# Expert down-projections of a mixture-of-experts block: from one fp32 product to three split fp32r products, two units later

## What is computed

```python
shared_out = silu(xf @ sw1) * (xf @ sw3) @ sw2
s = sigmoid(xf @ router_w.T)
_, topk_idx = top_k(s + router_bias, 2)
...
h = gelu(einsum('nd,edh->neh', xf, ew1), approximate=False)
y = einsum('neh,ehd->ned', h, ew2)
routed_out = einsum('ned,ne->nd', y, comb)
return (shared_out + routed_out).reshape(B, T, C)
```

## Time and profile before

| | us |
|---|---|
| median of 3 runs | 232.91 (232.39 to 233.5) |
| the profiled execution | 230.98 |
| its span, first to last instruction | 229.2 |
| PE busy | 207.9 (91%) |
| DVE busy | 157.3 (69%) |
| ACT busy | 137.9 (60%) |
| POOL busy | 107.5 (47%) |

### The profile page before, as it was taken

The page is one execution under the profiler, slowest core; times in us unless marked ns, Lnnn a source line. Parts: engine busy times, 40 slices in busy tenths (PEclk is TensorE's granted clock), DMA queues, the critical chain, the costliest instruction groups (busy, mean ns, idle before and its releaser), DMA issues.

```text
span 229.2 us, 4496 instructions
## 1 busy us (share of the span) xinstructions
PE 207.9 (91%) x1538; PEld 120.0 (52%) x1538; DVE 157.3 (69%) x333; ACT 137.9 (60%) x280; POOL 107.5 (47%) x208
## 2 busy tenths in 40 slices
PE   7998979989998989999899999899998999999970
PEld 7764555435564645546454554466664455645520
DVE  6688877849899899989994030664548655556654
ACT  2899464878877778778778877334341533534330
POOL 8787997023506379582965156144003802020203
PEclk9999955999999999999999999999999999999998
DMA  4391654384410000009000350000090010541011
GB/s 154 107 258 31 167 166 104 99 307 104 103 27 6 3 6 4 9 3 366 10 3 6 140 233 0 3 1 0 3 366 0 3 47 1 182 186 46 3 44 48
DMA packets 10422, 19.19 MB, mean 84 GB/s; under 512 B 1952, under 2 KB 7008, under 8 KB 9760
## 3 DMA queue, kind: packets, MB, share of 16 engines
q1 hardware_dynamic: 8976, 17.06, 22.7%
q10 hardware_dynamic: 1040, 1.05, 1.3%
q0 software_dynamic: 384, 0.79, 1.3%
HBM read 12.80 MB, written 1.11 MB: 61 GB/s over the span
## 4 chain that ended last, share of the span: by engine, by line
PE 68%; DVE 18%; ACT 7%; issue 4%; ACTq 1%; POOL 0%; POOLq 0%; DVEq 0%
PE ring L800 14%; PE pv_bank L826 10%; PE max_bank L960 9%; DVE top L672 8%; PE sum_bank L960 4%; PE ring L782 3%; PE ring L780 3%; PE ring L781 3%; ACT probs_mem L570 3%; PE max_bank L809 3%; PE pv_bank L834 2%; DVE hid L750 2%; PE misc_bank L882 1%; ACT xt L645 1%; PE misc_bank L780 1%
## 5 line engine op out<-in xcount | busy, mean ns | idle before, releaser
L672 DVE TENSOR_REDUCE top<-max_bank 128x2 f32<-128x512 f32 x128 | 81.0, 682 | 10.7 <-PE max_bank L809 10.4
L570 ACT ACTIVATE probs_mem<-ring 128x512 f32<-128x512 f32 x128 | 70.0, 596 | 19.4 <-PE ring L800 17.8
L800 PE MATMUL ring<-qstack,kstack 32*128 32x256 f32 x256 | 45.5, 336 | 6.4 <-ACT probs_mem L570 3.7
L809 PE MATMUL max_bank<-kstack,qstack 32*128 32x256 f32 x256 | 44.4, 338 | 1.1 <-DVE top L672 0.8
L800 PEld LDWEIGHTS ring<-qstack,kstack 32*128 32x128 f32 x256 | 29.3, 190 | 27.1 <-ACT probs_mem L570 16.1
L826 PE MATMUL pv_bank<-probs_mem,v 128*18 128x256 f32 x512 | 41.4, 397 | 0.4 <-ACT probs_mem L570 0.4
L750 DVE TENSOR_TENSOR hid<-xt,gates_mem 128x512 f32<-128x512 f32 x32 | 22.5, 703 | 24.0 <-ACT xt L645 24.0
L645 ACT ACTIVATE xt<-ring 128x512 f32<-128x512 f32 x32 | 19.1, 598 | 32.4 <-PE ring L782 32.4
L960 PE MATMUL max_bank<-hid,wf 128*128 128x512 f32 x60 | 32.0, 614 | 1.7 <-DVE hid L750 1.4
L809 PEld LDWEIGHTS max_bank<-kstack,qstack 32*128 32x128 f32 x256 | 28.3, 190 | 5.9 <-POOL kstack L475 1.8
L780 PE MATMUL ring<-yt_hi,wf_lo 128*128 128x512 f32 x40 | 31.3, 782 | 0.0
(11 more groups left out here) (191 smaller groups left out, 333.2 us busy)
## 6 DMA issues: line engine op xcount, KB each, us to landing
gates_mem<-gate_scratch SPq DMA_DIRECT2D x4, 2048.0 KB, 7.2
kstack<-gates_mem SPq DMA_DIRECT2D x36, 64.0 KB, 2.1
qstack<-gates_mem SPq DMA_DIRECT2D x24, 64.0 KB, 2.1
wf<-w_ffn_dram SPq DMA_DIRECT2D x1, 1408.0 KB, 6.3
xs<-x_dram SPq DMA_DIRECT2D x4, 256.0 KB, 5.4
xt<-x_t_dram SPq DMA_DIRECT2D x3, 256.0 KB, 4.4
qstack<-gates_mem POOLq DMA_DIRECT2D x12, 64.0 KB, 2.3
out_dram<-xs SPq DMA_DIRECT2D x3, 256.0 KB, 2.3
```

The lines of the kernel that those rows point to most:

```text
L570: nc.scalar.activation(probs[:, i % 2, s_heads(s)[r], :], ring_of(("scores", 2 * s + r))[:, :], ACT.Exp, scale=SCALE).then_inc(probs_made, 1)
L672: dve.tensor_reduce(top[:, m_heads(m)[r], t, :], max_bank[(2 * m + r) % NMAX][:, :].rearrange("p (h k) -> p h k", h=2), AX.X, ALU.max).the ...
L800: ins = mm(ring_of(("scores", 2 * s + r))[:, kt * S:(kt + 1) * S], kstack[rows, t, k:k + P], qstack[rows, t, b * S:(b + 1) * S], start=Tru ...
L809: ins = mm(max_bank[(2 * m + r) % NMAX][:, qt * S:(qt + 1) * S], qstack[rows, t, q:q + P], kstack[rows, t, b * S:(b + 1) * S], start=True, ...
```

## The change

Units 16 to 36 (`PARTED`) get a new job `parts`, in slot u + 1, and their down moves from slot u + 2 to slot u + 4. In `parts`, ACT copies `hid` of unit u to the fp32r buffer `hid_hi`, and POOL subtracts: `hid_lo` = `hid` - `hid_hi`. The down then is three fp32r products from these and from the split `ew2` (`e2_hi`, `e2_lo`), in place of one float32 product. `ew2` is split by POOL in eight pieces of 128 columns (`split e2`, slots 50 to 57). Of two jobs put in one slot the earlier put stands first, so in slot k ACT finds `parts` of unit k-1 ahead of the gelu of unit k. `hid` moves into the memory of `probs`, `hid_hi` and `hid_lo` into that of `kstack`, each four buffers. Units 37 to 39 and 0 to 15 keep the float32 down and the two slots. `accT`, `finT` and `norm2` of groups 1 and 2, whose last units (23 and 31) are parted, move two slots back.

```diff
+PARTED = range(NE + NG * NSH, NG * (NSH + NE) - 3)
+NPB = 4
+LAG, LAG_PARTED = 2, 4
...
+    for n in range(DOWN_PIECES):
+        put(18 + 2 * PIECES + n, ("split e2", n))
...
     for u in range(NUNITS):
         put(NHALF + u, ("unit", u))
-        put(NHALF + u + 2, ("down", u))
+        put(NHALF + u + (LAG_PARTED if u in PARTED else LAG), ("down", u))
+        if u in PARTED:
+            put(NHALF + u + 1, ("parts", u))
...
-        s = NHALF + last_of(g)
+        s = NHALF + last_of(g) + (LAG_PARTED - LAG if last_of(g) in PARTED else 0)
...
+        hid = probs_mem[:, 0:NHB * GT].rearrange("p (n t) -> p n t", n=NHB)
+        hid_hi, hid_lo = (kstack[:, i, 0:NPB * GT].rearrange("p (n t) -> p n t", n=NPB) for i in range(2))
...
+        def wait_hid_read(eng, u):
+            if u in PARTED:
+                eng.wait_ge(lo_made, u - PARTED.start + 1)
+            else:
+                eng.wait_ge(down_made, down_at[u])
...
+                    if kind == "split e2":
+                        c, e2 = slice(n * P, (n + 1) * P), slice(E2 + n * P, E2 + (n + 1) * P)
+                        pool.tensor_scalar(e2_hi[:, c], wf[:, e2], 1.0, None, ALU.mult).then_inc(e2_hi_made, 1)
+                        pool.wait_ge(e2_hi_made, n + 1)
+                        pool.tensor_tensor(e2_lo[:, c], wf[:, e2], e2_hi[:, c].bitcast(F32), ALU.subtract).then_inc(e2_split, 1)
+                    if kind == "parts":
+                        i = n - PARTED.start
+                        pool.wait_ge(hi_made, i + 1)
+                        pool.tensor_tensor(hid_lo[:, i % NPB, :], hid[:, n % NHB, :], hid_hi[:, i % NPB, :].bitcast(F32),
+                                           ALU.subtract).then_inc(lo_made, 1)
...
+                    if kind == "parts":
+                        wait_hid(act, b)
+                        n = b - PARTED.start
+                        if n == 0:
+                            act.wait_ge(pv_made, NHALF)
+                        if n >= NPB:
+                            act.wait_ge(down_made, down_at[b - NPB])
+                        nc.scalar.copy(hid_hi[:, n % NPB, :], hid[:, b % NHB, :]).then_inc(hi_made, 1)
...
+                        if b == 0:
+                            dve.wait_ge(pv_made, NHALF - 2)
                         if b >= NHB:
-                            dve.wait_ge(down_made, b - NHB + 1)
+                            wait_hid_read(dve, b - NHB)
...
+                        if b in PARTED:
+                            if b == PARTED.start:
+                                pe.wait_ge(e2_split, DOWN_PIECES)
+                            i = b - PARTED.start
+                            pe.wait_ge(lo_made, i + 1)
+                            c = slice((n - NSH) * P, (n - NSH + 1) * P)
+                            three(acc_bank[g][:, :], e2_hi[:, c], e2_lo[:, c], hid_hi[:, i % NPB, :], hid_lo[:, i % NPB, :],
+                                  False, b == last_of(g)).then_inc(down_made, 1)
```

More of the change, by code:

```diff
@@ L55 @@
 SPLIT = 512 + NE * P
+DOWN_PIECES = 8
 W1, W3, E1, W2, E2, RW = 0, 256, 512, 512 + NE * P, 512 + NE * P + 256, 512 + 2 * NE * P + 256
@@ L180, in build_layer @@
         rw_parts = sb("rw_parts", [P, 2, NE], F32R)
+        e2_hi = sb("e2_hi", [P, NE * P], F32R)
+        e2_lo = sb("e2_lo", [P, NE * P], F32R)
         ident = sb("ident", [P, P])
@@ L236, in build_layer @@
         comb_t = sb("comb_t", [NE, 2, S])
-        hid = sb("hid", [P, NHB, GT])
+        hid = probs_mem[:, 0:NHB * GT].rearrange("p (n t) -> p n t", n=NHB)
+        hid_hi, hid_lo = (kstack[:, i, 0:NPB * GT].rearrange("p (n t) -> p n t", n=NPB) for i in range(2))
         acc_t = xt[:, 0:GT]
@@ L274, in build_layer @@
         rw_split, w_hi_made, w_split = sem("rw_split"), sem("w_hi_made"), sem("w_split")
+        e2_hi_made, e2_split, hi_made, lo_made = sem("e2_hi_made"), sem("e2_split"), sem("hi_made"), sem("lo_made")
         up_made, act_made, sh_read, hid_dve, down_made = (
@@ L310, in build_layer @@
         staged = [u for u in uses if u[0] in ("q", "k")]
+        downs = [u for slot in slots for kind, u in slot.jobs if kind == "down"]
+        down_at = {u: n + 1 for n, u in enumerate(downs)}
         ring_uses = []
@@ L648, in _ @@
                         if t0 == 0:
-                            act.wait_ge(down_made, last_of(g) + 1)
+                            act.wait_ge(down_made, down_at[last_of(g)])
                             if g:
@@ L957, in _ @@
                                 pe.wait_ge(max_taken, 2 * NHALF)
[L958 to L961, removed]
+                        if b in PARTED:
[6 more added lines that the diff above has]
+                                  False, b == last_of(g)).then_inc(down_made, 1)
+                        else:
+                            wait_hid(pe, b)
+                            c = W2 + n * P
+                            mm(acc_bank[g][:, :], wf[:, c:c + P], hid[:, b % NHB, :], start=b == first_of(g),
+                               stop=b == last_of(g)).then_inc(down_made, 1)
                     if kind == "finT":
```

## The result

The kernel with the change takes 250.53 us (median of 6 runs, 247.82 to 252.63) against 233.2 (6 runs): a ratio of 1.0741, interval 1.067 to 1.0812. Its profiled execution took 247.82, with a span of 246.1, so 16.9 more than the 229.2 of before. Runs that were disturbed, on either side of a comparison, are left out of the ratios and of the times given for the experiments; the profiled executions of E1 and E2 were among them, and their stages are not read.

What follows compares the result with a forecast made beforehand. The bound was to move from PE to a loop through ACT, POOL and DVE of 2.53 us a unit: 16.0 to product 36 plus 1.2 at the end, 17.2 on 232.91, gives 250.1 us, range 237 to 254.

Steps and rivals of the forecast that it cites:

- rival A: Units 16 to 36: POOL's subtraction always precedes the next gate product, 2.53 us a unit; +17 us (15 to 20); chance 0.54.
- The loop: Gate product to next: hand-over 0.05, ACT copy 0.58, hand-over 0.08, POOL subtraction 1.27, product's remainder 0.55; 2.53 us a unit.
- The sum: Products 16 to 36 at 2.53 a unit, plus 0.5 net for finT and routing: product 36 ends 16.0 us later.
- B: POOL falls one unit behind after a delayed subtraction; loop 1.87, +5 us, 238; chance 0.30 with what lies between.
- The end: From product 36's end to the last down's start: 6.05 us instead of 4.86, so 1.2 more.
- C: PE's clock falls to its lower level because of idle time; 7 us more than rival A, 257; chance 0.08.
- Down as three products: PE, units 16 to 36: 0.85 becomes 0.72, gaining 0.13 us a unit, 2.7 us over 21 units, if PE sets the pace.
- The split of ew2: POOL's eight pieces, 8.8 us, mostly fit its waiting around y; one piece 1.1 late of 1.66 to spare; cost 0.
- A sign that was wrong: Units 17 to 36 of the profile after: the chain of waits goes through ACT, POOL and DVE; no size given.

Runs made afterwards that it cites:

- E1: Kernel before with only the float32 down of units 16 to 36 two slots later (lag of four), no split: 229.52 us, ratio 0.987 to before.
- E2: Changed kernel with ACT's copy and POOL's subtraction put behind the next unit in the slot: 238.64 us, ratio 1.028 to before.
- E5: Changed kernel with copy behind the next unit and POOL filling zeros instead of subtracting, low part of hid left out: 233.41 us, ratio 1.006 to before.
- E9: E5 with the transposes and load of group 3's gates (combT) two slots later: 232.72 us, ratio 1.007 to before.
- E3: Changed kernel with POOL's subtraction replaced by two zero fills that read nothing from SBUF, low part of hid left out: 238.96 us, ratio 1.028 to before.
- E10: E8 with the transposes and load of group 3's gates (combT) two slots later, full computation: 230.80 us, ratio 0.998 to before.
- E7: Kernel before with only the float32 down of units 16 to 36 one slot later (lag of three), no split: 229.47 us, ratio 0.989 to before.
- E4: Changed kernel with POOL's subtraction of 512 columns done as two of 256: 243.42 us, ratio 1.045 to before.
- E8: E2 with the subtraction on DVE, behind the product, instead of POOL, full computation: 234.18 us, ratio 1.011 to before.

## Why the prediction was right

Slower was forecast, by rival A, at a loop of 2.53 and 250.1 us; 250.53 came.

- **The loop.** The forecast had 0.05 + 0.58 + 0.08 + 1.27 + 0.55. The rows show 0.03 from product to copy, 0.69 from copy to subtraction (0.62 and 0.07), 1.27 and 0.54: 2.53. The copy from SBUF, bounded by 0.50 and 0.68, took 0.62 where 0.58 was put, and the hand-over from DVE less than was put. Unit spacings of 2.54 to 2.56 follow where nothing else disturbs.
- **The sum.** From the start of product 16 to the end of product 36 the forecast was 35.82 + 16.0 = 51.8; the rows give 231.26 - 179.26 = 52.0. From the end of product 17 on it is 48.68 against 19 x 2.53 = 48.07, so 0.6 where 0.5 net was put. That this size came out so well is luck: its parts, units from 1.87 to 2.99, were not worked out.
- **B, for short stretches.** It came as its condition had it, and after two units A was back, by the narrow margin worked out there. In after, DVE and POOL behind the last routing steps:

```profile
196.72 0.69 DVE L795 TENSOR_TENSOR probs_mem<-xt,gates_mem 128x512 f32<-128x512 f32 x1 [1.18 <-ACT xt L680]
198.59 0.72 DVE L795 TENSOR_TENSOR probs_mem<-xt,gates_mem 128x512 f32<-128x512 f32 x1 [1.18 <-ACT xt L680]
200.50 1.76 DVE L795 TENSOR_TENSOR probs_mem<-xt,gates_mem 128x512 f32<-128x512 f32 x1 [1.19 <-ACT xt L680]
...
197.48 4.24 POOL L504 TENSOR_TENSOR kstack<-probs_mem,kstack 128x512 fp32r<-128x512 f32 x3
```

POOL is one unit behind, two products take about 0.7 and stand 1.87 and 1.91 apart. The last of the three subtractions ends at 201.72, so with its usual 1.27 it started at about 200.45: 1.14 after the product that had ended at 199.31, where 1.12 was worked out. The product came at 200.50, 1.19 after, where 1.18 was. POOL was ahead by 0.05, and the product took 1.76. That the falls back to A come with products of 1.76 to 1.81 had not been put into the sum; with the shorter units of B they nearly cancel, as the 0.5 net allowed.

- **The end** was mis-sized: 1.2 was put, and from the end of product 36 to that of the last down it is 7.38 against 5.98, so 1.40. Product 39 did not follow 38 at once; it waited 0.46 for its gelu.
- **C** did not come on the pace of the units: from 215 to 230 the granted clock is 1.00 with PE idle for 5.9 of 15 us. The granted clock was 0.50, so 1.2 GHz, from about 209.5 to 213 and from 230 to 233.4, the first time just behind a wait of PE of 2.08 for the copy of an accumulator, the second time before such a wait, again of 2.08, was over. The argument against C, that the new gaps are shorter, was weaker than it looked: in the earlier trace rows the clock fell within the idle time of 1.40, not behind it. PE in after, at the first of them, and the window behind it:

```profile
209.13 0.77 PE L1020 MATMUL misc_bank<-ident,xt 128*128 128x128 f32 x4 [2.08 <-ACT xt L696]
```

```profile
210.00:215.00 5.00, 5.00 (x17) 3.93 (x17) 3.80 (x11) 2.18 (x5) 1.81 (x2) 0.71 0.00 0
```

The mean clock of 0.71 is part 1.2, part 2.4 GHz. The first fall cost nothing to speak of: the products of 211.09 and 216.14 are two units apart, 5.05 or 2.53 each, with the finT of group 1 between them. The second stands ahead of unit 39's up; that it made the 0.46 is likely, but no run took it away.

- **Down as three products** gives PE what was said and a little more: 1.39 a unit (E5) where 6 x 0.24 = 1.44 was put, against 1.57.
- **The split of ew2** was rightly taken at 0: y ended 0.6 later than before, at 127.31, and PE's transposes of it started at 127.73, still 0.42 behind it.
- **A sign that was wrong**: the chain was to go through ACT, POOL and DVE. It shows no POOL, for the reason given above.

The stages of the runs divide the loss. With the reads of POOL taken out, 50.64 becomes 38.80, so they cost 11.84; the copy ahead of the gelu is worth another 2.07 (E5), or 4.27 with `combT` moved (E9). E3, E5 and E9 have shorter POOL work besides, so that these shares hold the shorter work too. E10, which leaves nothing out of the computation, still comes to 32.81: the loss lies in the copy's place, the subtraction on POOL and the slot of `combT`, not in the three products.

What stays open: E10, with PE busy for 30.11 us of its stage where E7's is busy for 31.86, still needs 0.9 more. PE is idle for 2.70 there, and four of its waits, 2.07 together, are for the subtraction on DVE, but no run took these away. Why E2 missed its range by about 4 us is open too: its routing steps stand among POOL's subtractions as E5's do among the fills, so the waits found in E5 are likely there too, but that is not shown.

## What to carry to other kernels

Work that goes to an idle engine is priced by what that engine's memory reads do to the busy ones, and by where its wait stands in the other engines' order: here a copy put ahead of a gelu closed a loop through ACT, POOL and DVE, and PE's gain of 0.18 a unit could not count. In a profile an instruction that another engine holds up looks busy, not waiting; compare its duration with an undisturbed one of the same shape before reading the chain. And try the cheap half of a change by itself: the longer lag alone gave 1.1%, and with the split beside it, freed of its waits, nothing was left of that.

## What the runs showed that was not expected

- In these runs, who gets in is not symmetrical. A DVE product gets in between two POOL instructions in a run of them (E4: products of 0.69 beside 13 halves in a row); a POOL step stood behind four DVE instructions in a row (E8: 2.47 for 0.29, and the same in E10). The four leave no gap: each starts 0.08 ahead of the end of the one before it (189.05 against 188.45 + 0.68). That this is the reason is not shown.
- In E4 also the normalising step of DVE, which reads one tile from SBUF, was held up while POOL's halves ran, 10 in 8.59 us: 2.39 against 1.11 in after for the same four instructions. DVE, in E4 and then in after:

```profile
218.07 2.39 DVE L817 TENSOR_SCALAR xs<-xt,mv,rstd 128x128 f32<-128x128 f32 x4
```

```profile
223.37 1.11 DVE L815 TENSOR_SCALAR xs<-xt,mv,rstd 128x128 f32<-128x128 f32 x4
```
